# A fused delta-rule attention and spline feed layer on one core: a convolution tap moved to ScalarE, gate products moved behind the V blocks, and another order of loads in the feed part

## The reference

```
xn = layernorm(x)
# attention part, 6 heads, key width 64, value width 128
q, k, v = (silu(conv4(xn @ W)) for W in (Wq, Wk, Wv))   # causal convolution over 4 tokens, one set of taps per channel
beta = sigmoid(xn @ Wb);  g = -exp(A_log) * softplus(xn @ Wa + dt_bias)
for each token:                                         # S is 64 x 128 per head
    S = S * exp(g)
    S = S + outer(k, (v - k @ S) * beta)
    o = q @ S
o = o * rsqrt(mean(o*o) + eps) * norm_weight * silu(xn @ Wg)
attn = o @ Wo
# feed part: three 2048 x 512 weights, each a cubic spline through some 8000 control points
feed = (silu(xn @ gate_w.T) * (xn @ up_w.T)) @ down_w
out = x + attn + feed
```

## Time and profile before

| what | value |
|---|---|
| runs, median of 3 | 876.75 us (869.08, 876.75, 876.76) |
| profiled execution, its time | 871.43 us |
| its span, first to last instruction | 869.9 us |
| mean granted clock of TensorE in it | 0.953 of full |
| PE busy | 775.7 us, 89% |
| DVE busy | 574.6 us, 66% |
| ACT busy | 471.1 us, 54% |
| POOL busy | 384.8 us, 44% |
| DMA | 62.2 MB, 72 GB/s on average |

### The profile page before, as it was taken

How to read it: one execution, slowest core, us unless ns; L and a number is a source line. 1 busy time by engine, 2 the same in 40 slices (tenths; PEclk the granted TensorE clock), 3 DMA queues, 4 the chain that set the end, 5 groups by cost and what they waited for, 6 DMA issues and landing times.

```text
span 869.9 us, 15485 instructions
## 1 busy us (share of the span) xinstructions
PE 775.7 (89%) x5688; PEld 451.5 (52%) x5688; DVE 574.6 (66%) x1400; ACT 471.1 (54%) x1078; POOL 384.8 (44%) x419
## 2 busy tenths in 40 slices
PE   2989379998978999987999997899579999999998
PEld 1455157656547756645774655665124444444443
DVE  4889957768876778894877896568554544444400
ACT  3757746654875764685665486668553333333300
POOL 2376977567792655586355667022341000000000
PEclk9989789998989999898999899999799999999999
DMA  6502021330021031003023001054855222222011
GB/s 201 201 14 48 5 75 40 101 78 19 17 78 46 30 111 61 1 0 119 11 98 88 11 1 34 6 172 124 229 121 170 73 73 73 73 61 72 25 61 36
DMA packets 59936, 62.20 MB, mean 72 GB/s; under 512 B 30391, under 2 KB 45100, under 8 KB 59862
## 3 DMA queue, kind: packets, MB, share of 16 engines
q1 hardware_dynamic: 53526, 44.97, 18.3%
q0 software_dynamic: 4224, 13.11, 4.9%
q10 hardware_dynamic: 2112, 3.15, 1.1%
HBM read 33.69 MB, written 19.73 MB: 61 GB/s over the span
## 4 chain that ended last, share of the span: by engine, by line
PE 60%; DVE 14%; POOL 10%; issue 6%; SPq 5%; DMA 3%; ACT 2%; POOLq 0%; ACTq 0%; DVEq 0%
PE bank L643 14%; PE pd L1983 6%; PE pd L1984 6%; PE pd L1985 6%; SPq L423 5%; PE bank L729 3%; DVE cv L1040 2%; PE bank L803 2%; PE bank L720 2%; POOL cv L1627 2%; PE bank L855 2%; POOL rn L1608 1%; PE pg L1969 1%; PE bank L831 1%; DVE BA L1210 1%
## 5 line engine op out<-in xcount | busy, mean ns | idle before, releaser
L643 PE MATMUL bank<-x_parts,w 128*128 128x512 f16 x576 | 130.2, 384 | 1.5 <-DVE x_parts L997 1.5
L2055 DVE TENSOR_TENSOR hh<-sg,pu 128x512 f32<-128x512 f32 x64 | 43.9, 687 | 103.0 <-ACT sg L2022 90.7
L643 PEld LDWEIGHTS bank<-x_parts,w 128*128 128x128 f16 x576 | 56.2, 99 | 69.7 <-issue 6.9
L1927 POOL DMA_DIRECT2D yr<-y_attn x16 | 8.8, 553 | 185.2 <-DMA out<-yr 185.2
L643 PE MATMUL bank<-w,x_parts 128*128 128x384 f16 x384 | 77.1, 359 | 7.9 <-ACT V L1404 7.7
L2022 ACT ACTIVATE sg<-pg 128x512 f32<-128x512 f32 x64 | 38.0, 594 | 71.6 <-PE pg L1970 71.3
L643 PEld LDWEIGHTS bank<-w,x_parts 128*128 128x128 f16 x384 | 39.3, 107 | 39.0 <-issue 9.9
L1608 POOL TENSOR_TENSOR rn<-t,mhalf 128x6 f32<-128x6 f32 x16 | 22.8, 1424 | 73.6 <-DVE t L1203 73.6
L1040 DVE SCALAR_TENSOR_TENSOR cv<-raw,taps,cv 128x512 f32<-128x512 f32 x72 | 53.5, 808 | 0.0
L1983 PE MATMUL pd<-dw,it 128*128 128x512 f16 x128 | 48.8, 381 | 0.0
L1984 PE MATMUL pd<-dw,it 128*128 128x512 f16 x128 | 48.8, 381 | 0.0
(11 more groups left out here) (310 smaller groups left out, 2053.1 us busy)
## 6 DMA issues: line engine op xcount, KB each, us to landing
xb<-in_x SPq DMA_DIRECT2D x4, 1024.0 KB
xr<-in_x SPq DMA_DIRECT2D x16, 256.0 KB, 2.6
y_attn<-xr SPq DMA_DIRECT2D x16, 256.0 KB
down_rows<-inv SPq DMA_DIRECT2D x8, 512.0 KB, 5.8
yr<-y_attn POOLq DMA_DIRECT2D x16, 256.0 KB, 2.9
out<-yr SPq DMA_DIRECT2D x16, 256.0 KB, 2.0
xn_hi<-x_parts POOLq DMA_DIRECT2D x4, 512.0 KB
xn_lo<-x_parts POOLq DMA_DIRECT2D x4, 512.0 KB
```

The source lines that it names most:

```text
L643: ins = nc.tensor.matmul(out, a, b, start=first and i == 0, stop=last and i == 2)
L2055: v.tensor_tensor(hh[:, i % 2, :], sg[:, i % 2, :], pu[i % 2][:], ALU.mult).then_inc(h_ready, 1)
```

## The change

Four things are changed.

1. **Present tap.** In blocks 1 to 3 the last of the four q and k taps, that of the present token, is no longer added by DVE. ACT writes it to `cv` first (`present_tap`, one scaled copy of 512 columns, directly behind `raw_out` and the SiLU of two blocks before), and DVE adds the other three with three `scalar_tensor_tensor`. In block 0 DVE still does all four, present tap first.
2. **Clearing.** In blocks 1 to 3 `tin` is cleared by POOL, behind its last `masked_g` and ahead of the square root `nk` and the weight masks; DVE clears it in block 0 only. The waits for the stores that read `inv` move to POOL with it.
3. **Gate products of chunk 1 and the first V copies.** The two products `gate_products(s, 1, h)` and their SiLUs, which stood behind V blocks 0 and 1, stand behind `v_transposes(s, 1)`, ahead of `solve`, on PE, and behind `v_tokens(s, 1)` on ACT. On ACT `v_tokens(s, 0)` goes ahead of the SiLU of V block 4. The ring follows.
4. **Feed part.** Features 0 to 3 of the following block are made at i = 6..9, not 8..11. In the first block ACT's and DVE's share of the last turn comes at i = 4 and 5, not 1 and 2. On SP `load_x` of block 1 goes ahead of the moves 4 and 5, and `load_x` of block 2 goes behind the four moves of the following block, as do the later ones; the store of the first output tile of each block goes ahead of those moves, and the other three behind them.

```
 def bank_uses():
-    for n in range(NV):
-        ring += [("blk", NQK + n)] + (gates[2 + n:3 + n] if n < 2 else [])
-    ring += [("vtr", 0), ("vtr", 1), gates[4], ("vtr", 2), ("vtr", 3), gates[5], ("vtr", 4), ("vtr", 5)] + gates[6:]
+    ring += [("blk", NQK + n) for n in range(NV)]
+    ring += [("vtr", 0), ("vtr", 1), gates[2], gates[3], gates[4], ("vtr", 2), ("vtr", 3), gates[5], ("vtr", 4), ("vtr", 5)] + gates[6:]
...
 # tensor, local
-                    if n < 2:
-                        gate_products(s, 1, n)
                 v_transposes(s, 0)
...
                 v_transposes(s, 1)
+                for h in range(2):
+                    gate_products(s, 1, h)
                 solve(s)
...
 # vector, convolve
+                if s.first():
+                    for n in blocks:
...
+                        v.tensor_scalar(cv[:, n % 2, :], raw[:, n % 3, TAPS - 1:], P.taps[:, n, TAPS - 1:TAPS], None,
+                                        ALU.mult).then_inc(last_tap, 1)
+                for i in range(TAPS - 1):
                     for n in blocks:
                         if i == 0:
                             dve.wait_ge(raw_ready, s.val(NBLK, n + 1))
+                            dve.wait_ge(last_tap, s.val(NQK, n + 1))
...
+                        ins = v.scalar_tensor_tensor(out=out, in0=raw[:, n % 3, i:i + ST], scalar=P.taps[:, n, i:i + 1], in1=out,
+                                                     op0=ALU.mult, op1=ALU.add)
...
 # vector, invert_blocks
-                if not s.first():
-                    dve.wait_ge(downs.down_stored, 32 * s.idx())
-                if s.idx() >= 2:
-                    dve.wait_ge(samples.kept, 16 * (s.idx() - 1))
-                dve.wait_ge(t32_step, step(v.memset(tin, 0.0)))
-                cleared = step(v.memset(tin[:, 0:SUB * SUB:SUB + 1], 1.0))
+                if s.first():
+                    v.memset(tin, 0.0).then_inc(tin_cleared, 1)
...
+                dve.wait_ge(tin_cleared, s.val(2, 2))
...
 # scalar
+            def present_tap(s, n):
+                ready(act, ("blk", n), s)
+                act.wait_ge(silu_done, s.val(NBLK, n - 1))
+                sc.activation(cv[:, n % 2, :], raw[:, n % 3, TAPS - 1:], ACT.Copy, scale=P.taps[:, n, TAPS - 1:TAPS]
+                              ).then_inc(last_tap, 1)
...
 # scalar, local
                     raw_out(s, n)
+                    if n < 2 and not s.first():
+                        present_tap(s, n)
...
                         silu(s, n - 2)
+                        if not s.first():
+                            present_tap(s, n)
...
-                    if n < 2:
-                        gates(s, 1, n)
                     if n < NV - 1:
                         raw_out(s, NQK + n + 1)
+                    if n == NV - 1:
+                        v_tokens(s, 0)
                     if n >= 1:
                         silu(s, NQK + n - 1)
-                v_tokens(s, 0)
                 v_tokens(s, 1)
+                for h in range(2):
+                    gates(s, 1, h)
...
 # gpsimd, local
+                if not s.first():
+                    pool.wait_ge(downs.down_stored, 32 * s.idx())
+                    if s.idx() >= 2:
+                        pool.wait_ge(samples.kept, 16 * (s.idx() - 1))
+                    g_.memset(tin, 0.0).then_inc(tin_cleared, 1)
...
 # feed, sync
-            moves(0, range(HB, HB + 2))
             start.load_x(sp, At(None, 1))
-            moves(0, range(HB + 2, NP))
+            moves(0, range(HB, NP))
...
                 if s >= 1:
                     moves(s, range(HB, NP))
+                    store(At(None, s - 1), 0)
+                if s < nst - 1:
+                    moves(s + 1, range(HB))
                 if s < nst - 2:
                     start.load_x(sp, At(None, s + 2))
...
 # feed, tensor
-                    if following is not None and 8 <= i < 8 + HB:
-                        start.features(pe, following, i - 8, pf[i % 2])
+                    if following is not None and 6 <= i < 6 + HB:
+                        start.features(pe, following, i - 6, pf[i % 2])
...
 # feed, scalar (vector alike, with 9 -> 7 and i == 2 -> i == 5)
-                    if following is not None and 9 <= i < 9 + HB:
-                        start.feature_hi(act, following, i - 9, pf[(i - 1) % 2])
+                    if following is not None and 7 <= i < 7 + HB:
+                        start.feature_hi(act, following, i - 7, pf[(i - 1) % 2])
...
-                    if s.first() and i == 1:
+                    if s.first() and i == 4:
                         start.turned_high(act, TURNS - 1, pd[0])
```

More of the change, by code:

```diff
@@ L1025, in convolve @@
             def convolve(s, blocks):
-                for i in range(TAPS):
+                if s.first():
+                    for n in blocks:
+                        dve.wait_ge(raw_ready, s.val(NBLK, n + 1))
+                        if n >= 2:
+                            dve.wait_ge(silu_done, s.val(NBLK, n - 1))
+                        v.tensor_scalar(cv[:, n % 2, :], raw[:, n % 3, TAPS - 1:], P.taps[:, n, TAPS - 1:TAPS], None,
+                                        ALU.mult).then_inc(last_tap, 1)
+                for i in range(TAPS - 1):
                     for n in blocks:
@@ L1030, in convolve @@
                             dve.wait_ge(raw_ready, s.val(NBLK, n + 1))
[L1031 to L1037, removed]
+                            dve.wait_ge(last_tap, s.val(NQK, n + 1))
                         else:
                             dve.wait_ge(dve_step, last[n])
-                            ins = v.scalar_tensor_tensor(out=out, in0=src, scalar=w, in1=out, op0=ALU.mult, op1=ALU.add)
-                        if i < TAPS - 1:
+                        out = cv[:, n % 2, :]
+                        ins = v.scalar_tensor_tensor(out=out, in0=raw[:, n % 3, i:i + ST], scalar=P.taps[:, n, i:i + 1], in1=out,
+                                                     op0=ALU.mult, op1=ALU.add)
+                        if i < TAPS - 2:
                             last[n] = steps.next()
@@ L1096, in step @@
                     return t32.next()
-                if not s.first():
-                    dve.wait_ge(downs.down_stored, 32 * s.idx())
-                if s.idx() >= 2:
-                    dve.wait_ge(samples.kept, 16 * (s.idx() - 1))
-                dve.wait_ge(t32_step, step(v.memset(tin, 0.0)))
-                cleared = step(v.memset(tin[:, 0:SUB * SUB:SUB + 1], 1.0))
+                if s.first():
+                    v.memset(tin, 0.0).then_inc(tin_cleared, 1)
+                    dve.wait_ge(tin_cleared, 1)
+                    v.memset(tin[:, 0:SUB * SUB:SUB + 1], 1.0).then_inc(tin_cleared, 1)
                 dve.wait_ge(diag_ready, s.val(NCH, NCH))
@@ L1668, in local @@
                         samples.gather(pool, range(12 + c, 13 + c))
+                if not s.first():
[3 more added lines that the diff above has]
+                    g_.memset(tin, 0.0).then_inc(tin_cleared, 1)
+                    pool.wait_ge(tin_cleared, s.val(2, 1))
+                    g_.memset(tin[:, 0:SUB * SUB:SUB + 1], 1.0).then_inc(tin_cleared, 1)
                 ready(pool, ("sums",), s)
@@ L1778, in _ @@
                 load_x(s, b)
-                sp.wait_ge(t32_step, b.val(T32_STEPS, 3))
+                sp.wait_ge(t32_step, b.val(T32_STEPS, 1))
                 for c in range(2):
@@ L1907, in _ @@
                 if s >= 1:
-                    store(At(None, s - 1), 0)
-                    store(At(None, s - 1), 1)
-                if s < nst - 1:
-                    moves(s + 1, range(HB))
-                if s >= 1:
-                    store(At(None, s - 1), 2)
-                    store(At(None, s - 1), 3)
+                    for t in range(1, NCH):
+                        store(At(None, s - 1), t)
             for t in range(NCH):
@@ L2078, in groups @@
                         start.feature_lo(dve, s, HB + i - 1, pf[(i - 1) % 2])
-                    if following is not None and 9 <= i < 9 + HB:
-                        start.feature_lo(dve, following, i - 9, pf[(i - 1) % 2])
-                    if s.first() and i == 2:
+                    if following is not None and 7 <= i < 7 + HB:
+                        start.feature_lo(dve, following, i - 7, pf[(i - 1) % 2])
+                    if s.first() and i == 5:
                         start.turned_low(dve, TURNS - 1, pd[0])
```

17 lines of the change are left out of this document (8 added, 9 removed).

## The result

The changed kernel is **slower**: median 878.94 us of 19 runs (874.67 to 889.97) against 870.42 us of 19 runs of before (864.32 to 879.27), a ratio of **1.0107, with a 95% interval of 1.0081 to 1.0133**, or +9.3 us on 873.5. The ratio is of runs in the faster of two states alone; the run of the changed kernel at 889.97 is not among them. The profiled execution took 878.79 us with a span of 877.2. Both kernels spread over some 15 us, so ratios and not single runs are compared.

A forecast was written before the change was run, and what follows sets the result against it. PE was taken as busiest everywhere, with its waits for POOL, ACT, DVE, moves and gathers deciding. Gains of 2.1 + 1 + 2.5 = 5.6 us off the mean 873.5 gave 867.9 us, with an eight-in-ten range of 859 to 877.

The forecast's parts named there:

- the term of the gate products and V copies: V blocks, blocks 1 to 3: 2.5 us gained less 1.7 for low clock, taken as 1 us gain.
- the price of the low clock: Products behind the V blocks: 3.4 us at low clock costs 1.7 us, counted in one of three blocks.
- Present tap and clearing: q and k taps: 2.1 us gain over three blocks, ends 0 and 3.5; clearing moved to POOL: 0.
- My allowance for POOL's collision there: Second block's taps: POOL's masked_g may slow DVE's additions, half a microsecond more lost; gain taken as 1.4 us.
- Feed part: Feed part: second block's gate_up some 6 us sooner, 3 or more given back at down; gain 2.5 us, ends 0 and 8.5.
- the new wait for `dw`: Feed part, second block: PE waits for gathers before a down, giving back 3 us or more of 6.
- the rival by which the gathers don't bind: Feed part: gathers land 3 us sooner, so the gain is 8.5 us; time 862 us, chance 0.20.
- a load ahead that delays the moves: Feed part: 1 MB issued first leaves the last move no sooner; feed gain 0, time 870.4 us, chance 0.20.
- gain at the V blocks: V blocks, blocks 1 to 3: moved products let V blocks come sooner, 1.15 us net in the second; 2.5 in sum at 2.4 GHz.
- the clock, whole: slower: Behind the V blocks: three products at 1.2 GHz throughout, 4.9 us lost per block; time 883.6 us, chance 0.06.

The follow-up runs named there:

- the filled kernel: The changed kernel with PE transposing V block 1 six times over, same place and values, in the wait ahead of the moved gate products; ratio 0.9993 to before.
- gates_alone: The kernel before with only the gate products of chunk 1, the ring and the V copies moved; ratio 1.0138 to before, +12.0 us.
- no_gates_copies: The changed kernel with the gate products where they were, but the V copies moved as in the change; ratio 0.9933 to before, -5.8 us.
- after_wait: The changed kernel with POOL's second addition of V block 0 in the first block waiting for DVE's spline coefficients; ratio 1.0038 to before.

## Why the prediction was wrong

The time of 868 us was wrong in sign, and the measured one lies above the range of 859 to 877. The step that failed is the term of the gate products and V copies, which I put at a gain of 1 us (ends +4 and -15); alone it costs **12.0 us** (7.6 to 16.5). Within it, the price of the low clock was counted in one block of three, and the first block was put at nothing without a reason. The other terms held.

**Present tap and clearing.** Forecast a gain of 2.1 us and 0; measured together 1.8 (-1.0 to 4.6), an interval that includes no gain, so it is the trace that bears this out. The wait at the second block's scores fell by 2.1 us, to 0.41. My allowance for POOL's collision there (a gain of 1.4, not 2.5) was too careful. DVE's transpose still waited for ACT's `diag`, now 1.54 us, as forecast.

**Feed part.** Forecast 2.5 us; measured 1.5 (-1.5 to 4.4), again not clear of none. Both waits for moves shrank as I had said, the new wait for `dw` came where I had put it (4.09 us, last gather issued at 660.09), and the rival by which the gathers don't bind is out. So is the other, a load ahead that delays the moves: the first wait fell from 6.82 to 3.57.

**Gate products.** Two things were wrong in one term, and one was right.

First, the **clock**. I had the right rows, and the right stretch, 3.4 us of idle PE (it was 3.72), and charged one block in three. In the profiled execution all three blocks were hit: 6.75, 6.98 and 6.82 us for two products, 2.7 to 2.9 us each above the 4.07 of the filled kernel, 8.3 in three. The row I had read as an example (one product at 4.02 behind a wait) was the rule: in before that happened in the second and third blocks and partly in the fourth. The cure bears it out: with the wait filled, the products run in 4.07 us and the kernel is 9.9 us faster, 6.7 more than the same fill brings before. The rest of the reckoning for this place was right: from the first V product to the end of gate product (2,0) the second block took 36.7 us before (220.28 to 256.99), I forecast 1.15 less, and the filled kernel took 35.8 (223.16 to 258.91); the changed one took 38.4 (218.54 to 256.94).

Second, the **first block**. I had left it out without a line. Its solve waits 12.9 us for DVE's inversion, and the change brings POOL's V additions forward there as well (`eg` at 80.55 for 82.05, and at 79.77 in `gates_alone`), into DVE's preparation, ahead of that inversion. Four steps of 0.23 to 0.43 us became 1.25 to 1.53 in `gates_alone`, the clearing came 3.6 us later, and so did the solve (114.88 for 111.27). Over all traces the clearing starts at 82.6 to 85.6 (mean 84.1) in the eight kernels with the products where they were, at 85.7 to 89.8 (mean 88.1) in the five with them moved, and at 82.5 to 82.8 in the three in which POOL is held back. Holding it back gave 5.7 us in one kernel, 6.0 in another and 9.7 in the third, each with an uncertainty of 4 to 6 either way. The Trainium skill ("SBUF — State Buffer", "Who interferes with whom") states the rule that I cited for the taps, where it hardly mattered, and did not apply here: whoever has the shared port pair keeps it for the whole instruction. The trace agrees, since the long DVE steps end 0.15 to 0.3 us behind POOL's additions.

Third, the **gain** that these were to be set against was right: POOL's last V addition ahead of the copies ended 28.6 us behind the first V product in the second block (247.16), 2.3 us sooner than the 31.0 of before (251.23). It was simply small.

The sum of the parts: two products at low clock -8.3, first block -3.6 (profile) to -6 (runs), gain at the V blocks +2.5 as forecast, is -9 to -12, against the 12.0 measured. That it comes near is in part luck: it leaves out the stretches of the next paragraph, so how the 12.0 divide isn't shown. The rival "the clock, whole: slower" gave 883.6, and 873.5 times the ratio is 882.8; but it got there with three products at 1.2 GHz per block, and the runs show two of them and the first block. Its number was nearly right, its mechanism half.

**What stays open** is the 14 us at half clock in the recurrence, some 5 us each: from gate product (2,0) to the product behind (3,0) the changed kernel took 20.3 us in the second block (254.82 to 275.07) and 25.4 in the third (394.53 to 419.92). Such a stretch stood in at least one block of each of the six unfilled traces with the moved products, in different blocks. Of the six unfilled ones without them only `no_gates_copies` had any (two), and none of the four filled ones had. So they don't need the moved products but come far more often with them; what brings them on was not found. The 9.9 us of the fill may hold their absence as much as the quick products. The total points the same way: over the first 600 us, by windows of 1 us, TensorE stood at half clock for 51 to 75 us in the six unfilled traces without the moved products, 72 to 92 in the six with them, and 34 to 48 in the four filled ones. The low clock behind a part of PE's waits is shown; the division between the moved products and the recurrence is not.

## What to carry to other kernels

Before you put work behind a wait of the matrix engine, look at the clock of what stands behind that wait now: if it already runs at half speed, what you add there may run so too (24 matmuls took 6.75 us here for 4.07), and in every block, not in one. When an off-path engine is made earlier, go through each block of the program, the first too, and ask which engine's work it now collides with, above all where that other engine is the one waited for. Keep the idle engine busy with useless work, as a test, in the kernel before as well: what the fill brings only after the change is what the clock costs it.

## What the runs showed that I had not expected

Useless work made a kernel faster: 20 more transposes a block, 2.2 us of them at 2.4 GHz (2.78 for 24, 0.60 for 4), brought 3.2 us in the kernel before (0 to 6) and 9.9 in the changed one.

The collision of DVE and POOL in the first block differs between executions: the same program started the clearing at 85.68 in one and at 88.89 in another; with POOL held back (`after_wait`) it was 82.77. Those 3.2 us can be a part of the spread over runs of one kernel, but not the most of it: the 12 runs of `after_wait` still spread over 11 us.
